# Expert retrieval: the mask products of a chunk issued in two halves, one group of expert rows behind each half

## The chip, the cores and the metric

The kernel runs on one core of one Trainium2 chip. The metric is the device time of one execution in microseconds (us), lower is better. Three runs of the kernel before took 1929.24 us in the median (1924.55 to 1931.2).

## The reference, cut to what matters

The whole program is four layers on x of shape 2 x 1024 x 256 (2048 tokens, 256 features); each layer adds `ffn(cond(x))` to x. The change touches only the feed-forward part of layer 0, a retrieval from 4096 experts by product keys:

```
q = (rmsnorm(x) @ w_q.T)                        # 8 heads, two halves of 128
s1, i1 = top_k(sim with keys half 0, 8)         # per token and head
s2, i2 = top_k(sim with keys half 1, 8)
fs, pk = top_k(s1[:, None] + s2[None, :], 8)    # 8 of 64 sums
fi = i1 * 64 + i2 at pk                         # 64 experts per token in all
hidden = gelu(xn . expert_down[fi]) * relu(fs)
out = sum over the 64 of hidden * expert_up[fi]
```

Nothing is gathered in this kernel. For each block of tokens all 4096 products with `expert_down` are taken, passed through gelu, and multiplied by a matrix of weights that is zero but for the 64 chosen experts of a token; a dense product with `expert_up` follows.

## The kernel before, in words

The program is a row of stages, each a block of code for every engine, one after the other. The stage of the change is `peer`. It walks over 8 blocks of 256 tokens (NPB = 8, PB = 256). Of a block there are:

- *Expert rows* (`act_rows`, L430 to L438, TensorE): the 4096 products per token, 32 slices j of 128 experts. Two slices are a *group* (16 groups, NGRP). The group is 4 matmuls in the source and 8 pairs of weight load and matmul in the trace, since each fp32 matmul is two. They use the whole array, 128x128, with 256 columns. ScalarE takes gelu of a group from one of two PSUM buffers into `hg` (L508).
- *Mask products* (`weigh`, L440 to L453, TensorE): the matrix of weights. A *chunk* is 16 token pairs (PAIRS), 8 chunks a block (CHUNKS), so 2 groups to a chunk (GPC). For each pair, the one-hot masks `am` and `bm` are contracted over the 64 slots of a token on quarters of the array, 64x64 with 32 columns: 64 matmuls in the source, 128 pairs of load and matmul in the trace. The result lies in `ps_w`, which has a single buffer.
- *Masks*: VectorE builds `bm` and `am` by comparison (`build`, L650 and L652) three chunks ahead in a ring of four; GpSimd multiplies `bm` by the slot's weight (L563).
- *The multiplication by the weights*: VectorE multiplies 1024 elements of `hg` per partition by the whole of `ps_w` once a chunk (L682) and signals `p_done`.
- *Up product* (L474, TensorE): 64 matmuls in the source, 128 pairs in the trace, 128x128 with 256 columns, then the sum with x on VectorE (L658).
- *Routing* of a later block: `scores` (L416, TensorE), `pick` (L584 to L639, VectorE), `turn` (two transposes, L426 and L427) and `keep` (ScalarE, L514 to L516), after which `build` may read the slots.

The order on each engine is written out by hand; semaphores tie them. TensorE in `work(i)` goes through the chunks of block i: before a chunk's mask products it waits for `a_done`, `b_done` (the masks) and `p_done` (L444: the multiplication of the chunk before has read `ps_w`), adds to a semaphore that marks the start (L445), issues the mask products, signals `w_ready`, and then issues two groups of the expert rows of block i + 1. After chunk 7 it issues the scores of block i + 2 (where there is one), waits for the last `p_done` and issues the up product. VectorE, per chunk: build the masks of three chunks later, then wait for `w_ready` and multiply. In block 0 it also does two parts of `pick` of block 1 in each chunk, and TensorE has the scores of block 1 behind chunks 0 and 4. In blocks 1 to 5 `pick` runs during the up product. Block 6 has no routing left, and block 7 no expert rows: there only mask products stand between the waits. Blocks 1 to 4 are two turns of a hardware loop; the others are written out.

Of the kernel before, what the change touches and what calls it, by code (L numbers as in the profile page):

```python
# [66 lines left out]
class Stage:  # L67
# [18 lines left out]
    def sem(self, name):  # L86
        return self.ctx.enter_context(self.nc.semaphore(f"{self.name}_{name}"))
# [253 lines left out]
PAIRS = 16  # L341
# [3 lines left out]
CPT = CHUNKS // PT  # L345
RING = 4
NGRP = NJ // 2
GPC = NGRP // CHUNKS


def peer(nc, a, g):
# [7 lines left out]
    with Stage(nc, "peer") as st:  # L359
# [31 lines left out]
        a_done, beq_done, b_done = sem("a_done"), sem("beq_done"), sem("b_done")  # L391
        w_begun, w_ready, p_done, o_ready, x_done = sem("w_begun"), sem("w_ready"), sem("p_done"), sem("o_ready"), sem("x_done")
# [3 lines left out]
        @block.sync  # L396
        def _(sp):
            def load_x(i):
                sp.dma_start(xin[:], a["x"][:, :, bass.ds(i * PB, PB)]).then_inc(xload, 16)

            load_x(0)
            with sp.Fori(1, NPB) as r:
                sp.wait_ge(x_done, r)
                load_x(r)

        @block.tensor
        def _(pe):
            def scores(i, t):

                n = i * PT + t  # L410
                if t == 0:
                    pe.wait_ge(xt_done, i + 1)
                pe.wait_ge(sim_read, n)
                for h in range(2):
                    for c in range(C):
                        mm = pe.matmul(ps_s[:, h, :], xt[:, c, t * P:(t + 1) * P],  # L416
                                       g.key_map[:, c, h * BLK:(h + 1) * BLK], start=(c == 0), stop=(c == C - 1))
                mm.then_inc(sim_ready, 1)

            def turn(i, t):  # L420

                n = i * PT + t
                pe.wait_ge(codes_done, n + 1)
                pe.wait_ge(kept, n * 6)
                flat = codes[:].rearrange("p a k -> p (a k)")
                pe.transpose(ps_t[:, 0:P], flat[:, 0:P], g.ident[:])  # L426
                pe.transpose(ps_t[0:SLOTS, P:2 * P], flat[:, P:P + SLOTS], g.ident[:]).then_inc(turned, 1)  # L427

            def act_rows(i, group):

                n = i * NGRP + group
                pe.wait_ge(gelu_done, n)
                for r in range(2):
                    j = 2 * group + r
                    for c in range(C):
                        mm = pe.matmul(ps_h[group % 2][:, r, :], down[:, c, j * P:(j + 1) * P],  # L436
                                       g.x[:, c, bass.ds(i * PB, PB)], start=(c == 0), stop=(c == C - 1))
                mm.then_inc(h_ready, 1)  # L438

            def weigh(i, c):  # L440
                n = i * CHUNKS + c
                pe.wait_ge(a_done, n + 1)
                pe.wait_ge(b_done, n + 1)
                pe.wait_ge(p_done, n + 1)  # L444
                pe.sem_inc(w_begun, 1)  # L445
                for m in range(PAIRS):
                    for k in range(P // WC):
                        of = slice(WC * k, WC * k + WC)
                        for z in range(2):
                            token = slice(64 * z, 64 * z + 64)  # L450
                            mm = pe.matmul(ps_w[of, z, m, :], am[c % RING][token, m, of], bm[c % RING][token, m, :],  # L451
                                           start=True, stop=True)
                mm.then_inc(w_ready, 1)  # L453

            def work(i, half, first=False, more=True, route=True):

                for c in range(CHUNKS):
                    weigh(i, c)
                    if more:
                        if first and c % CPT == 0:  # L460
                            scores(i + 1, c // CPT)
                        for group in range(c * GPC, (c + 1) * GPC):
                            act_rows(i + 1, group)
                            if first and group == NGRP // 2 + 1:
                                turn(i + 1, 0)
                            if not first and group == 2:
                                turn(i + 1, 1)
                if route:
                    scores(i + 2, 0)
                pe.wait_ge(p_done, i * CHUNKS + CHUNKS + 1)  # L470
                pe.wait_ge(x_done, i)
                for c in range(C):
                    for j in range(NJ):
                        mm = pe.matmul(ps_o[:, c, :], up[:, j, c * P:(c + 1) * P], hg[half][:, j, :],  # L474
                                       start=(j == 0), stop=(j == NJ - 1))
                        if c == 0 and j == NJ // 2 and first:
                            turn(i + 1, 1)
                        if c == 0 and j == NJ // 2 and route:
                            scores(i + 2, 1)
                        if c == 1 and j == 2 and route:  # L480
                            turn(i + 2, 0)
                mm.then_inc(o_ready, 1)

            scores(0, 0)
            for group in range(NGRP):
                act_rows(0, group)
                if group == 3:
                    scores(0, 1)
                if group == 5:
                    turn(0, 0)  # L490
            turn(0, 1)
            work(0, 0, first=True)
            with pe.Fori(0, NPB // 2 - 2) as r:
                work(r * 2 + 1, 1)
                work(r * 2 + 2, 0)
            work(NPB - 3, 1)
            work(NPB - 2, 0, route=False)
            work(NPB - 1, 1, more=False, route=False)
# [1617 lines left out]
```

## Time and profile before

| what | us |
|---|---|
| median of three runs | 1929.24 |
| the profiled execution's own time | 1929.26 |
| its span | 1927.6 |
| TensorE busy | 1757.1 (91%) |
| TensorE weight loads busy | 1097.1 (57%) |
| VectorE busy | 943.0 (49%) |
| ScalarE busy | 374.6 (19%) |
| GpSimd busy | 305.4 (16%) |
| stretch of the stage, first mask product to the end of the last sum | 194.7 to 853 |

The table says how busy each engine is over the whole span, which is a mean over stages with different limits. What counts here is the stretch from 194.7 to about 853 us, and in it the stretches in which the mask products and the expert rows alternate. Loads and matmuls of TensorE are two rows of the trace (PEld and PE) that overlap, and matmul ends are modelled; starts are better to reckon with than busy times. A row's first number is its start from the begin of the span, the second how long the merged instructions last from the first start to the last end.

### The profile page before, as it was taken

What the parts mean: (1) busy time and instruction counts of PE and PEld (TensorE: products, weight loads), DVE (VectorE), ACT (ScalarE), POOL (GpSimd) and SP (SyncE); (2) the same over time, 40 slices, a digit from 0 to 9 for tenths busy, and PEclk for the clock granted to TensorE, in tenths of its full rate; (3) what the DMA queues carried; (4) which work ended last, traced back from release to release, by engine and by line L of the source; (5) the groups of instructions that cost most, each with busy time, mean ns of one, the idle gap of its engine ahead of it and who ended that gap; (6) DMA issues with size and microseconds to landing.
All of it is one profiled execution on the core that took longest, in us unless ns stands there. A gap on an engine that the chain in (4) does not pass through costs nothing. (4 is left out here: it accounts for less than half of the span.)

```text
span 1927.6 us, 32039 instructions
## 1 busy us (share of the span) xinstructions
PE 1757.1 (91%) x13350; PEld 1097.1 (57%) x13350; DVE 943.0 (49%) x2520; ACT 374.6 (19%) x635; POOL 305.4 (16%) x150
## 2 busy tenths in 40 slices
PE   5879789999999999778799998999999976998998
PEld 2347678887888888764344443444444455447443
DVE  1326888768687785407311111111114497236676
ACT  2222111120111201001011111111113639133200
POOL 0000413151331514200394000000000000004000
PEclk9988899999999999789899999999999988999999
DMA  7000000000000000025310001200001044000000
GB/s 305 33 0 6 2 2 8 2 9 8 2 8 2 9 7 3 8 79 232 150 47 1 0 0 73 123 0 0 0 0 55 0 155 139 6 0 1 6 17 22
DMA packets 20043, 73.33 MB, mean 38 GB/s; under 512 B 3530, under 2 KB 8130, under 8 KB 17090
## 3 DMA queue, kind: packets, MB, share of 16 engines
q1 hardware_dynamic: 19906, 71.37, 9.9%
q8 instruction: 102, 1.67, 0.4%
q14 instruction: 35, 0.29, 0.0%
HBM read 69.26 MB, written 2.10 MB: 37 GB/s over the span
## 5 line engine op out<-in xcount | busy, mean ns | idle before, releaser
L563 POOL TENSOR_TENSOR peer_bm<-peer_bm,peer_slots 128x512 f32<-128x512 f32 x64 | 193.9, 3029 | 609.1 <-DVE peer_bm L650 609.1
L436 PE MATMUL peer_ps_h<-all_x,layer_down 128*128 128x256 f32 (+1 forms) x1024 | 241.3, 390 | 0.4 <-issue 0.4
L474 PE MATMUL peer_ps_o<-peer_hg,layer_up 128*128 128x256 f32 x1024 | 226.6, 382 | 1.5 <-DVE peer_hg L682 1.5
L474 PEld LDWEIGHTS peer_ps_o<-peer_hg,layer_up 128*128 128x128 f32 x1024 | 195.9, 192 | 33.3 <-issue 5.2
L436 PEld LDWEIGHTS peer_ps_h<-all_x,layer_down 128*128 128x128 f32 x1024 | 192.9, 193 | 28.4 <-issue 2.5
L1129 DVE SCALAR_TENSOR_TENSOR skills_hid<-skills_ps_u,all_pair_w,skills_act_g 128x512 f32<-128x512 f32 x64 | 48.0, 751 | 294.7 <-PE skills_ps_u L1091 294.7
L451 PE MATMUL peer_ps_w<-peer_bm,peer_am 64*64 64x32 f32 x8192 | 144.5, 227 | 31.9 <-DVE peer_hg L682 25.1
L451 PEld LDWEIGHTS peer_ps_w<-peer_bm,peer_am 64*64 64x64 f32 x8192 | 137.1, 144 | 52.1 <-issue 52.1
L508 ACT ACTIVATE peer_hg<-peer_ps_h 128x512 f32<-128x512 f32 x128 | 76.4, 597 | 371.7 <-PE peer_ps_h L436 371.7
L652 DVE TENSOR_TENSOR peer_am<-all_iota_a,peer_slots 128x2048 f32<-128x2048 f32 x64 | 146.2, 2285 | 0.0
L1108 ACT ACTIVATE skills_act_g<-skills_ps_g 128x512 f32<-128x512 f32 x96 | 57.3, 597 | 438.0 <-PE skills_ps_g L1091 438.0
L1091 PE MATMUL skills_ps_u<-all_x,skills_w 128*128 x256 | 120.3, 593 | 0.0
L1091 PE MATMUL skills_ps_g<-all_x,skills_w 128*128 x256 | 120.3, 593 | 0.0
L1078 PE MATMUL skills_acc<-skills_hid,skills_w 128*128 128x512 f32 x256 | 120.0, 593 | 0.0
L682 DVE TENSOR_TENSOR peer_hg<-peer_ps_w,peer_hg 128x1024 f32<-128x1024 f32 x64 | 78.2, 1222 | 77.6 <-PE peer_ps_w L451 77.5
L1310 POOL PARTITION_ALL_REDUCE quant_alltop<-quant_top x5 | 2.1, 424 | 588.9 <-DVE quant_top L1214 588.9
L1129 DVE SCALAR_TENSOR_TENSOR skills_hid<-skills_ps_u,skills_act_g 128x512 f32<-128x512 f32 x32 | 22.1, 692 | 142.5 <-PE skills_ps_u L1091 142.5
L1091 PEld LDWEIGHTS skills_ps_g<-all_x,skills_w 128*128 128x128 f32 x256 | 48.8, 191 | 61.1 <-issue 61.1
L1078 PEld LDWEIGHTS skills_acc<-skills_hid,skills_w 128*128 128x128 f32 x256 | 48.8, 191 | 61.1 <-issue 61.1
L1091 PEld LDWEIGHTS skills_ps_u<-all_x,skills_w 128*128 128x128 f32 x256 | 48.8, 191 | 61.1 <-issue 61.1
L1326 PE MATMUL quant_ps_m<-layers_y,layer_qw 128*128 128x512 f32 x192 | 82.8, 593 | 0.7 <-ACT layer_qw L1369 0.7
L1091 PE MATMUL skills_ps_g<-all_x,four_skill 128*128 x128 | 63.7, 622 | 17.2 <-DMA four_skill<-in_skills 10.7
(288 smaller groups left out, 2228.0 us busy)
## 6 DMA issues: line engine op xcount, KB each, us to landing
quant_w<-in_l_w SPq DMA_DIRECT2D x64, 256.0 KB, 4.3
lora_w<-in_l_w SPq DMA_DIRECT2D x8, 1024.0 KB, 8.7
four_skill<-in_skills SPq DMA_DIRECT2D x2, 3072.0 KB, 12.9
skills_w<-in_skills SPq DMA_DIRECT2D x2, 3072.0 KB, 15.1
skills_w<-in_skill_shared SPq DMA_DIRECT2D x2, 3072.0 KB, 22.0
layer_down<-in_down SPq DMA_DIRECT2D x1, 4096.0 KB, 24.3
layer_up<-in_up SPq DMA_DIRECT2D x1, 4096.0 KB, 33.5
swiglu_w<-in_cond SPq DMA_DIRECT2D x2, 1541.0 KB, 8.2
```

Source lines behind the costliest of these rows:

```text
L436: mm = pe.matmul(ps_h[group % 2][:, r, :], down[:, c, j * P:(j + 1) * P], g.x[:, c, bass.ds(i * PB, PB)], start=(c == 0), stop=(c == C - 1))
L451: mm = pe.matmul(ps_w[of, z, m, :], am[c % RING][token, m, of], bm[c % RING][token, m, :], start=True, stop=True)
L474: mm = pe.matmul(ps_o[:, c, :], up[:, j, c * P:(c + 1) * P], hg[half][:, j, :], start=(j == 0), stop=(j == NJ - 1))
L508: act.activation(hg[half][:, 2 * group:2 * group + 2, :], ps_h[group % 2][:], ACT.Gelu).then_inc(gelu_done, 1)
L563: pool.tensor_tensor(bm[c % RING][:], bm[c % RING][:], slots[half][:, 2, c * PAIRS:(c + 1) * PAIRS].unsqueeze(2).to_broadcast([P, PAIRS, WJ]),
L652: dve.tensor_tensor(am[c % RING][:], g.iota_a[:].unsqueeze(1).to_broadcast([P, PAIRS, P]), slots[half][:, 0, col].unsqueeze(2).to_broadcas ...
L682: dve.tensor_tensor(acts, ps_w[:].rearrange("p z m j -> p z j m"), acts, ALU.mult).then_inc(p_done, 1)
L1078: mm = pe.matmul(acc[k][c][:], w_down[s][:, m, c * P:(c + 1) * P], hid[j % 4][:], start=(s == 0 and m == 0), stop=(s == 2 and m == M2 - 1))
L1091: mm = pe.matmul(bank[:], weight[:, c, m * P:(m + 1) * P], g.x[:, c, bass.ds((b * BPB + k) * BLK, BLK)], start=(c == 0), stop=(c == C - 1))
L1108: act.activation(act_g[j % 2][:], ps_g[j % 2][:], ACT.Gelu_apprx_tanh).then_inc(gelu_done, 1)
L1129: dve.scalar_tensor_tensor(out=hid[j % 4][:], in0=ps_u[j % 2][:], scalar=scale, in1=act_g[j % 2][:], op0=ALU.mult, op1=ALU.mult).then_inc( ...
L1326: mm = pe.matmul(ps_m[n % n_ring][:], wt[z][:, c, m * P:(m + 1) * P], g.y[:, c, q * BLK:(q + 1) * BLK], start=(c == 0), stop=(c == C - 1))
```

## The change

`weigh` takes a `part`, 0 or 1. Part 0 has the waits, the mark of the start and the mask products of pairs 0 to 7; part 1 has the products of pairs 8 to 15 and the signal `w_ready`. In `work`, part 0, one group, part 1, one group take the place of all products and two groups. The scores in block 0 move from behind the whole of a chunk's products to behind part 0. The number of instructions that TensorE computes with is as before, and so is all code of the other engines.

```diff
-            def weigh(i, c):
+            def weigh(i, c, part):
                 n = i * CHUNKS + c
-                pe.wait_ge(a_done, n + 1)
-                pe.wait_ge(b_done, n + 1)
-                pe.wait_ge(p_done, n + 1)
-                pe.sem_inc(w_begun, 1)
-                for m in range(PAIRS):
+                if part == 0:
+                    pe.wait_ge(a_done, n + 1)
+                    pe.wait_ge(b_done, n + 1)
+                    pe.wait_ge(p_done, n + 1)
+                    pe.sem_inc(w_begun, 1)
+                for m in range(part * PAIRS // GPC, (part + 1) * PAIRS // GPC):
...
-                mm.then_inc(w_ready, 1)
+                if part == GPC - 1:
+                    mm.then_inc(w_ready, 1)
...
                 for c in range(CHUNKS):
-                    weigh(i, c)
-                    if more:
-                        if first and c % CPT == 0:
-                            scores(i + 1, c // CPT)
-                        for group in range(c * GPC, (c + 1) * GPC):
+                    for part in range(GPC):
+                        group = c * GPC + part
+                        weigh(i, c, part)
+                        if more:
+                            if first and c % CPT == 0 and part == 0:
+                                scores(i + 1, c // CPT)
                             act_rows(i + 1, group)
                             if first and group == NGRP // 2 + 1:
                                 turn(i + 1, 0)
                             if not first and group == 2:
                                 turn(i + 1, 1)
```

## Rows read from the trace of the kernel before

**Rows 1.** The page's 40 slices: TensorE's busy tenths and granted clock.
```profile
PE   5879789999999999778799998999999976998998
PEclk9988899999999999789899999999999988999999
```

**Rows 2.** Busy time by stretch: chunks of block 0, of block 2, of block 7.
```profile
core 0: us, PE busy (x) PEld busy (x) DVE busy (x) ACT busy (x) POOL busy (x), PEclk, DMA share, GB/s
194.70:273.40 78.70, 64.31 (x1179) 50.80 (x1179) 69.60 (x209) 11.89 (x24) 30.30 (x10) 0.89 0.01 2
385.40:430.53 45.13, 45.13 (x1155) 39.57 (x1155) 33.14 (x28) 10.66 (x22) 24.23 (x8) 1.00 0.03 9
786.22:822.25 36.03, 23.20 (x1025) 22.39 (x1024) 21.44 (x17) 0.00 (x0) 12.12 (x4) 0.68 0.04 11
```

**Rows 3.** Waits of TensorE's matmuls, blocks 1 to 6: total, times, longest.
```profile
PE peer_ps_w L451 <- issue: 4.0, 4, 1.8
PE peer_ps_w L451 <- DVE peer_hg L682: 0.9, 1, 0.9
```

**Rows 4.** Timeline of one chunk, block 2: start, length, engine, line, idle before.
```profile
402.57 1.97 PEld L451 LDWEIGHTS peer_ps_w<-peer_bm,peer_am 64*64 64x64 f32 x128 [0.33 <-issue]
404.58 3.32 PEld L436 LDWEIGHTS peer_ps_h<-all_x,layer_down 128*128 128x128 f32 x16
404.71 1.23 DVE L682 TENSOR_TENSOR peer_hg<-peer_ps_w,peer_hg 128x1024 f32<-128x1024 f32 x1 [1.62 <-PE peer_ps_w L451]
405.85 0.68 DVE L650 TENSOR_TENSOR peer_bm<-all_iota_a,peer_slots 128x512 f32<-128x512 f32 x1
406.45 2.29 DVE L652 TENSOR_TENSOR peer_am<-all_iota_a,peer_slots 128x2048 f32<-128x2048 f32 x1
408.23 1.96 PEld L451 LDWEIGHTS peer_ps_w<-peer_bm,peer_am 64*64 64x64 f32 x128 [0.33 <-issue]
...
425.18 1.96 PEld L451 LDWEIGHTS peer_ps_w<-peer_bm,peer_am 64*64 64x64 f32 x128 [0.33 <-issue]
```

**Rows 5.** The sequencer's wait and mark of that chunk, 403 to 408.2 us.
```profile
L444 PEldq EVENT_SEMAPHORE  x1: 51/51/51, 406.0 to 406.0; - x1
...
L445 PEldq EVENT_SEMAPHORE  x1: 51/51/51, 406.1 to 406.1; - x1
```

**Rows 6.** Timeline, up product of block 6 and first chunks of block 7.
```profile
758.29 27.60 PEld L474 LDWEIGHTS peer_ps_o<-peer_hg,layer_up 128*128 128x128 f32 x128
786.22 1.96 PEld L451 LDWEIGHTS peer_ps_w<-peer_bm,peer_am 64*64 64x64 f32 x128 [0.33 <-issue]
788.43 1.23 DVE L682 TENSOR_TENSOR peer_hg<-peer_ps_w,peer_hg 128x1024 f32<-128x1024 f32 x1 [1.34 <-PE peer_ps_w L451]
789.94 1.99 PEld L451 LDWEIGHTS peer_ps_w<-peer_bm,peer_am 64*64 64x64 f32 x128 [1.76 <-issue]
```

**Rows 7.** Timeline, a chunk of block 7 at the lower clock.
```profile
801.70 3.54 PEld L451 LDWEIGHTS peer_ps_w<-peer_bm,peer_am 64*64 64x64 f32 x128 [1.64 <-issue]
```

**Rows 8.** Timeline of block 0, chunks 1, 4 and 5.
```profile
208.15 2.85 PEld L451 LDWEIGHTS peer_ps_w<-peer_bm,peer_am 64*64 64x64 f32 x118 [4.67 <-issue]
212.18 5.00 PEld L436 LDWEIGHTS peer_ps_h<-all_x,layer_down 128*128 128x128 f32 x16
214.43 1.21 DVE L682 TENSOR_TENSOR peer_hg<-peer_ps_w,peer_hg 128x1024 f32<-128x1024 f32 x1
...
242.27 1.15 DVE L584 MAX8 peer_s<-peer_ps_s 128x8 f32<-128x64 f32 x8 [5.92 <-PE peer_ps_s L416]
...
245.41 0.27 PE L426 MATMUL peer_ps_t<-all_ident,peer_codes 128*128 128x128 f32 x1
...
247.62 0.69 DVE L650 TENSOR_TENSOR peer_bm<-all_iota_a,peer_slots 128x512 f32<-128x512 f32 x1 [2.03 <-ACT peer_slots L516]
```

**Rows 9.** Timeline, first chunk of the hardware loop's second turn.
```profile
469.15 0.66 PEld L451 LDWEIGHTS peer_ps_w<-peer_bm,peer_am 64*64 64x64 f32 x34 [1.89 <-issue]
```

**Rows 10.** Timeline, last sum of the stage and first load of the next.
```profile
852.39 0.69 DVE L658 TENSOR_TENSOR all_x<-peer_ps_o,peer_xin 128x512 f32<-128x512 f32 x1 [30.19 <-PE peer_ps_o L474]
853.56 0.34 SPq L768 DMA_DIRECT2D lora_a_rows<-in_l_a  x1
```

## The prediction

> **What bounds the kernel now.** I read the page's slices first. TensorE's digits are 9 over most of the retrieval stage, from the sixth slice to the sixteenth, with a granted clock of 9 tenths or more [rows 1]. The busy time by stretch then tells which part of the stage has slack. In the chunks of block 2 TensorE's matmul row is busy for 45.13 of 45.13 us at clock 1.00, VectorE for 33.14. In block 0 VectorE is busy 69.60 of 78.70 us and TensorE 64.31, at clock 0.89. In block 7, without expert rows, neither is full [rows 2]. The waits say the same: over blocks 1 to 6 TensorE's mask products wait 4.0 us for issue and 0.9 us for VectorE, in 480 us [rows 3]. So in blocks 1 to 6 whatever lengthens TensorE's stream lengthens the kernel, and a wait that is taken away would give nothing, since there is none. Nor does a later stage take it up: the next stage's first load is issued at 853.56 us, after the stage's last sum at 852.39 [rows 10].
>
> Last, the timeline of one chunk [rows 4]. A chunk begins with its first mask load at 402.57 us; the next begins at 408.23 and the fourth after it at 425.18: (425.18 - 402.57) / 4 = 5.652 us a chunk. How much of that is the products themselves?
> - Mask products: 128 loads in 1.96 us, the last of which lasts about 0.135, so one starts every (1.96 - 0.13) / 127 = 0.0144 us, and 128 take 1.84 us.
> - Expert rows: the up product has the same shape, and its 128 loads take 27.60 us [rows 6], so (27.60 - 0.19) / 127 = 0.2158 us each, and 16 take 3.45 us.
> - Together 5.30 us. The remaining 0.36 us (5.652 - 1.843 - 3.453 = 0.356) is what it costs to go from expert rows to mask products and back, once a chunk. On the way in the loads stand still for 0.33 us; on the way out the first expert load comes at 404.58, about 0.17 after the last mask load, and the second one a little early, which gives some back.
>
> **The change part by part.**
>
> *The added pair of edges, blocks 1 to 6.* The chunk was products, two groups; it becomes half, group, half, group. Each chunk with expert rows gets one more edge of each kind. That is 6 blocks x 8 chunks = 48 pairs in the part where TensorE sets the time. What does an added pair cost? The trace has no edge without the waits ahead of it, so I bound it. Lower end: nothing, and even 0.1 us of gain if only the early second load remained. Upper end for the edge: the 0.36 us of today. I take 0.356. The reason: the sequencer passes the wait for `p_done` at 406.0 us and the mark at 406.1 [rows 5], while the mask loads that follow start at 408.23. It is 2.1 us ahead, so neither wait nor mark holds up the loads; the 0.33 us is the array's own, between 128x128 work and 64x64 work. The same 0.33 us stands ahead of block 7's first mask products, behind the up product [rows 6]. 48 x 0.356 = 17.1 us.
>
> The Trainium skill, page "TensorEngine Tiling (Array Packing)", section "Key Properties", has a rule that speaks against this change: changing the tiling mode, not just the tile, drains the TensorE. By it the added edges cost as much as the present ones, since no wait is part of their price; the trace's equal gaps agree. If instead the gap were the waits', the added edges would be nearly free, and that is a rival below.
>
> *The wait for `p_done` gets closer.* Now two groups lie between the end of the products and the next ones; afterwards one. Queued behind the wait are the mask products, and behind them everything of TensorE. The multiplication starts 0.13 us after the first expert load (404.71 against 404.58) and takes 1.23; where TensorE waits for it, in block 7, the mask loads start 789.94 - (788.43 + 1.23) = 0.28 us after its end [rows 4, 6]. So with one group the loads can start at the earliest 0.13 + 1.23 + 0.28 = 1.64 us after the group's first load. The group itself and the edge take 1.73 + 0.2 = 1.92. The wait is hidden with 0.28 us to spare. The mask loads lose the sequencer's lead of 2.1 us; if the lead were needed whole, a chunk would be 3.65 - 1.92 = 1.73 us longer, 83 us in all. But in block 7 they start with no lead and take 1.99 against 1.96 [rows 6]: 0.03 us. 48 x 0.03 = 1.4 at most; I take 0.5. Behind chunk 7 of block 6 there are no scores to cover the wait before the up product: 1.64 against 1.62, nothing.
>
> VectorE can be in time: its cycle is 1.23 + 0.68 + 2.29 = about 4.1 us, and it idles 1.62 us before each multiplication [rows 4], which now comes in a cycle of 6.0.
>
> *Block 0.* VectorE's chain sets the time, and its cycle of about 7.7 us or more covers the added edges where TensorE runs at the upper clock (half 0.9, group 1.7, half 0.9, edges 0.7: 4.3 us from `p_done` to `w_ready`, against 6.3 us until VectorE wants it). At the lower one (1.2 GHz) it doesn't. 128 mask loads take 3.54 us there [rows 7], and 8 expert rows 2 x 1.73 = 3.5. In chunk 1 the products start at 208.15 us, with a stall inside; now they end at about 212, afterwards at 208.15 + 3.5 + 3.5 + about 0.6 of edges = 215.8, and the multiplication, at 214.43 today, comes at about 216 [rows 8]. +1.5 us. In chunk 4 the path runs through TensorE to the transposes at 245.41 and by ScalarE to the build at 247.62, which VectorE waits for 2.03 us: both halves, both groups and the scores all lie before them, so the added pair counts: +0.4. The scores come half a chunk's products earlier and shorten the 5.92 us wait, but the build behind them waits for the transposes anyway: 0. I take +2 for the block, bounds 0 (lower clock in other places) and +5 (three chunks like chunk 1).
>
> *Loop edge.* At the loop's second turn the mask products stall 1.89 us for issue after 94 loads [rows 9]. A group behind half of them gives the instructions more time to arrive. Four such stalls cost 4.0 us [rows 3]; bounds 0 to -4, and I take -1.
>
> *Block 7 and the up products*: same instructions in the same order, 0.
>
> **Sum**: 17.1 + 0.5 + 2 - 1 = 18.6 us, on 1929.26 of the profiled execution, which is the median of the runs (1929.24) to 0.02: 1947.9, say 1948 us, 1.0% slower. Likeliest case's own range: 1943 (block 0 at 0, stalls at -3.5) to 1953 (block 0 at +5, lead at 1.4).
>
> **The rivals.**
> - *Half a price.* Only one direction of the edge repeats: the way out (about 0.16 us of the 0.36) is plain, the way in is tied to the start of a chunk. 48 x 0.18 = 8.6, plus 1: 1939 us. For it: no edge without a wait is in the trace. Against it: the sequencer is long past the start of the chunk when the loads stand still [rows 5]. 8%.
> - *The wait takes over.* If `p_done` to mask loads took 0.6 us rather than 0.28 when the sequencer has been held, the slack of 0.28 would be gone and 0.3 us a chunk added: 48 x 0.3 = 14 more, 1962 us. It decides from 0.56 us up. Against: block 7's row, the very case. 5%.
> - *The gap is the waits' after all*, and added edges cost nothing: 1929 us, with block 0 and the stalls cancelling. 4%.
> - *Faster, by shorter bursts.* Mask products issue an instruction every 7 ns, and a burst of half the length gives issue time to catch up: the stalls (4.0 us) go [rows 3], and in chunk 4 of block 0 VectorE's wait of 5.92 us shortens by half of 3.54 us, 1.8. 1929.3 - 5.8 = 1923.5. It wins only if an added pair costs under 5.8 / 48 = 0.12 us. For it: the rows of stalls. Against: 0.36 stands in each chunk at full rate, with no stall. 3%.
> - The forecast: 80%.
>
> **How the numbers follow.** Range 1938 to 1954: it takes in the forecast with its bounds and the half price, and leaves out 1962, 1929 and 1923.5, 12%, and some of the tails. A measurement of this kernel can't tell less than about 0.3% (5.8 us) from no change. Slower by more than that: 80 + 8 + 5 = 93%; within it: 4%; faster: 3%.
>
> **What would show it.** Right: in the timeline of blocks 1 to 6 the mask loads come in runs of 64, an idle of 0.33 us ahead of both runs, an expert group of 8 loads between them, and the next chunk 6.01 us after; TensorE's wait for L682 stays near nothing there; blocks 1 to 6 are 17 us longer. Wrong: an idle of 0.1 or less ahead of the second run (half price or none); a wait for L682 in each chunk (the wait took over); chunk period at 5.65. Block 0 wrong if its chunks 0 to 7 take less than 78.7 us or over 84.

## The result and the profile after

The changed kernel takes 1945.01 us in the median of five runs (1942.3 to 1949.53), the kernel before 1929.24 (also five). The ratio, over all runs, is 1.009 with a 95% interval of 1.0069 to 1.0111: slower by 13 to 21 us. The forecast was 1948 us, range 1938 to 1954. The profiled execution is the median one, 1945.01 us with a span of 1943.3.

The page's slices, as in [rows 1]; the sixth to sixteenth lie in the stage:

```profile
PE   5878799999999999879799998999999977998998
PEclk9988899999999999888899999999999988998899
```

The eye finds nothing there. TensorE was at 9 before and is at 9 now; that is what a stream made longer by small gaps looks like in busy tenths, since matmul ends are modelled and cover the gaps. The stretches answer to [rows 2]: the chunks of block 0, of block 2, of block 7.

```profile
194.97:274.12 79.15, 64.83 (x1179) 48.50 (x1179) 69.73 (x210) 11.89 (x24) 30.30 (x10) 0.91 0.01 2
388.57:439.53 50.96, 50.96 (x1162) 41.16 (x1162) 33.32 (x28) 11.27 (x23) 24.23 (x8) 1.00 0.03 9
798.24:835.71 37.47, 25.22 (x1025) 24.36 (x1025) 21.69 (x17) 0.00 (x0) 12.12 (x4) 0.61 0.04 10
```

Block 2's row is from its first mask load to its first up product; in the kernel before that stretch is 385.40 to 433.75, 48.35 us (it holds also the 3.2 us of scores that [rows 2] leave out). So +2.6 us in 8 chunks, with clock and matmul count the same. Block 0 has +0.5 us, block 7 +1.4 at a clock of 0.61 against 0.68. Block 7's chunks took 36.03 and 34.87 us in two traces of the kernel before, and 37.25 in experiment 4, where their order is unchanged too, so its 1.4 us can't be put down to the change.

The timeline of one chunk (start, length, engine, line), to be laid beside [rows 4]:

```profile
403.74 1.02 PEld L452 LDWEIGHTS peer_ps_w<-peer_bm,peer_am 64*64 64x64 f32 x64 [0.33 <-issue]
404.80 1.59 PEld L436 LDWEIGHTS peer_ps_h<-all_x,layer_down 128*128 128x128 f32 x8
404.94 1.22 DVE L685 TENSOR_TENSOR peer_hg<-peer_ps_w,peer_hg 128x1024 f32<-128x1024 f32 x1 [1.95 <-PE peer_ps_w L452]
...
406.73 1.02 PEld L452 LDWEIGHTS peer_ps_w<-peer_bm,peer_am 64*64 64x64 f32 x64 [0.33 <-issue]
407.79 1.59 PEld L436 LDWEIGHTS peer_ps_h<-all_x,layer_down 128*128 128x128 f32 x8
409.72 1.02 PEld L452 LDWEIGHTS peer_ps_w<-peer_bm,peer_am 64*64 64x64 f32 x64 [0.33 <-issue]
```

The load at 403.74 is part 1 of a chunk, the one at 406.73 part 0 of the next, the one at 409.72 that chunk's part 1. Both stand behind an idle of 0.33 us, though part 1 has no wait ahead of it. A chunk takes 2 x (406.73 - 403.74) = 5.98 us against 5.65. The multiplication ends at 404.94 + 1.22 = 406.16 and part 0 could load from 406.44 on (+0.28, [rows 6]); it does at 406.73. The wait for `p_done` is hidden with 0.29 us left. In the later chunks of block 7 the loads follow the multiplication's end by 0.22 and 0.23 us, which would leave 0.35. The sequencer shows the lead that is gone: it passes the last wait at 406.2 and the mark at 406.3 (in [rows 5] it was 2.1 us ahead, now 0.4).

```profile
L445 PEldq EVENT_SEMAPHORE  x1: 51/51/51, 406.2 to 406.2; - x1
...
L446 PEldq EVENT_SEMAPHORE  x1: 51/51/51, 406.3 to 406.3; - x1
```

**Where the time went.** The chunks of blocks 1 to 6, first mask load to first up product, add up to 305.3 us after and 294.0 before: only 11.3 us. Block 5 of the first trace explains why that isn't 15.7, the 48 added pairs of edges at 0.328 us each (experiment 2). Its row, and the same block in a second trace of the unchanged kernel (see the last experiments):

```profile
629.02:681.38 52.36, 50.30 (x1163) 42.43 (x1163) 33.25 (x29) 11.26 (x23) 24.23 (x8) 0.97 0.03 8
```
```profile
630.80:679.31 48.51, 48.39 (x1162) 41.04 (x1162) 33.14 (x29) 11.27 (x23) 24.24 (x8) 1.00 0.03 9
```

The 3.9 us of a stall and the lower clock behind it do not belong to the order of instructions, since they aren't there again. Against the second trace the six blocks have 305.3 - 290.1 = 15.2 us more. Block 0 gives 0.3 to 0.5. Block 7 and all behind it move by some 1 to 3 us either way from trace to trace, of one kernel too.

### The profile page after: what moved, and what is told of

It reads as the page before. It is cut to its first block and busy times, and to the rows that moved or that the text cites. A ratio compares the mean times of both kernels' runs of the same rounds, so it can differ in the third digit from the quotient of the medians.

```text
span 1943.3 us, 32039 instructions
## 1 busy us (share of the span) xinstructions
PE 1781.0 (92%) x13350; PEld 1098.5 (57%) x13350; DVE 943.9 (49%) x2520; ACT 374.7 (19%) x635; POOL 305.6 (16%) x150
## 5 line engine op out<-in xcount | busy, mean ns | idle before, releaser
L436 PE MATMUL peer_ps_h<-all_x,layer_down 128*128 128x256 f32 (+1 forms) x1024 | 253.9, 393 | 0.0
L436 PEld LDWEIGHTS peer_ps_h<-all_x,layer_down 128*128 128x128 f32 x1024 | 187.3, 191 | 27.7 <-issue 1.9
L452 PE MATMUL peer_ps_w<-peer_bm,peer_am 64*64 64x32 f32 x8192 | 153.8, 227 | 29.2 <-DVE peer_hg L685 27.2
L1094 PE MATMUL skills_ps_g<-all_x,four_skill 128*128 x128 | 63.9, 624 | 17.1 <-DMA four_skill<-in_skills 10.6
```

The costliest lines, as they stand in the source:

```text
L1094: mm = pe.matmul(bank[:], weight[:, c, m * P:(m + 1) * P], g.x[:, c, bass.ds((b * BPB + k) * BLK, BLK)], start=(c == 0), stop=(c == C - 1))
```

## The experiments

**1. The waits without the edge.** In the kernel before, the waits and the mark a second time, in the middle of the products:

```diff
                 for m in range(PAIRS):
+                    if m == PAIRS // 2:
+                        pe.wait_ge(a_done, n + 1)
+                        pe.wait_ge(b_done, n + 1)
+                        pe.wait_ge(p_done, n + 1)
+                        pe.sem_inc(w_begun, 1)
```

> The kernel before, with a second set of the three waits and the mark in the middle of each chunk's mask products, and no expert rows there: TensorE's waits without a change of the array's mode. Theory (the gap of 0.33 us is the array's switch between 128x128 and 64x64 work): the 128 mask loads still come in one run of 1.96 us, a chunk stays at 5.65 us, 1929 us in all. Rival (the gap belongs to the waits and the mark ahead of the products): an idle of about 0.3 us in the middle of each run, 64 x 0.3 = 19 us in all, of which the 48 chunks of blocks 1 to 6 count in full: 1944 us or more.

Measured: 1934.22 us against 1928.51, ratio 1.0027 (1.0008 to 1.0046). The timeline, block 2:

```profile
400.16 1.83 PEld L456 LDWEIGHTS peer_ps_w<-peer_bm,peer_am 64*64 64x64 f32 x117 [0.33 <-issue]
402.25 0.31 PEld L456 LDWEIGHTS peer_ps_w<-peer_bm,peer_am 64*64 64x64 f32 x11 [0.26 <-issue]
402.60 3.32 PEld L436 LDWEIGHTS peer_ps_h<-all_x,layer_down 128*128 128x128 f32 x16
406.25 1.96 PEld L456 LDWEIGHTS peer_ps_w<-peer_bm,peer_am 64*64 64x64 f32 x128 [0.33 <-issue]
```

The run of 128 loads is unbroken at its middle, as at 406.25, and the edge ahead of it is what it was. The next chunk's first load comes at 411.90, 5.65 us after 406.25. The waits alone don't make the gap: the rival is out. They aren't quite free, though. The program is slower by 1.5 to 9 us, and single bursts lose a little elsewhere, as the 0.26 us behind load 117. Of the 5.7 us between the medians, block 0 has 1.7 in the trace (80.50 against 78.80 in the second trace of the kernel before) and blocks 1 to 6 have 2.0 (292.1 against 290.1). That the extra sequencer instructions do it by the supply of instructions is a guess.

**2. Twice the added edges.** The products in parts of 6, 5 and 5 pairs. `GAPS` names, behind each part, the group of the chunk and its slices:

```diff
+CUTS = (0, 6, 11, 16)
+GAPS = (((0, (0,)),), ((0, (1,)),), ((1, (0, 1)),))
...
-                for m in range(part * PAIRS // GPC, (part + 1) * PAIRS // GPC):
+                for m in range(CUTS[part], CUTS[part + 1]):
```

> The mask products of a chunk in three parts (6, 5 and 5 pairs), half a group of expert rows behind the first and the second, one whole group behind the third. Two added pairs of edges a chunk instead of one, and the same distance to the wait for p_done as in the changed kernel. Theory (each pair of edges costs 0.33 us whatever stands between): chunks of 5.65 + 2 x 0.33 = 6.30 us, 48 x 0.65 = 31 us, and 1 to 2 us in block 0: 1961 us. Rival (the cost is that of splitting at all, or of the waits, and not of each edge): 1945 us, as the changed kernel. Rival (cost by the length of what stands between, as if an interrupted stream had to refill): less than 0.33 for the short gaps, 1950 to 1955 us.

Measured: 1960.11 us against 1928.51, ratio 1.0148 (1.0116 to 1.0181). Block 2:

```profile
394.69:448.28 53.59, 53.59 (x1162) 41.22 (x1162) 33.32 (x28) 11.27 (x23) 24.22 (x8) 1.00 0.03 8
```
```profile
407.52 0.79 PEld L456 LDWEIGHTS peer_ps_w<-peer_bm,peer_am 64*64 64x64 f32 x48 [0.33 <-issue]
408.36 0.73 PEld L439 LDWEIGHTS peer_ps_h<-all_x,layer_down 128*128 128x128 f32 x4
409.42 0.67 PEld L456 LDWEIGHTS peer_ps_w<-peer_bm,peer_am 64*64 64x64 f32 x40 [0.33 <-issue]
```

48.34, 50.96, 53.59 us for none, one and two added pairs a chunk: steps of 2.62 and 2.63, that is 0.328 us a pair, behind 4 expert loads as behind 8 or 16. The cost is by the edge, and not by how many expert loads lie between. Block 0 took 81.63 us, 2.9 more than in the kernel before, where 1 to 2 were expected: with two added pairs VectorE's chain no longer covers them.

What stands directly ahead of the edge does matter. Behind the two transposes, which have 128 columns where the expert rows have 256, the idle is 0.20 us:

```profile
404.58 0.11 PEld L429 LDWEIGHTS peer_ps_t<-all_ident,peer_codes 128*64 128x64 f32 x1
404.88 0.67 PEld L456 LDWEIGHTS peer_ps_w<-peer_bm,peer_am 64*64 64x64 f32 x40 [0.20 <-issue]
```

And where the work changes but the 128x128 shape stays, there is no gap. In the kernel before, the last expert loads of block 6 end at 754.94 + 3.32 = 758.26 us and the up product loads from 758.29 [rows 6]:

```profile
754.94 3.32 PEld L436 LDWEIGHTS peer_ps_h<-all_x,layer_down 128*128 128x128 f32 x16
```

So the gap goes with the change from 128x128 to 64x64. Whether it is a price of the change itself, or the rest of the last wide product that the next load can't overlap, no run separates.

**3. The same edges, the wait brought too close.** The whole group first, half a group behind the last part. The edit against experiment 2:

```diff
-GAPS = (((0, (0,)),), ((0, (1,)),), ((1, (0, 1)),))
+GAPS = (((0, (0, 1)),), ((1, (0,)),), ((1, (1,)),))
```

> The same parts and the same number of edges as the thirds with the long gap last, but the whole group behind the first part and half a group behind the second and the third, so that only half a group stands between the last product and the wait for p_done. Theory: the mask loads can start at the earliest 1.64 us after the half group's first load (0.13 until the multiplication, 1.23 for it, 0.28 until the loads), and the half group takes 0.54 + 0.52 = 1.06: TensorE waits 0.58 us for L685's like in 7 of 8 chunks, 42 x 0.58 = 24 us more than the other thirds, 1985 us. Rival (the sequencer's lead matters beyond the wait itself, so that mask loads run slower when it is gone): more than 24 us, and loads further apart than 14 ns in a part. Rival (the wait has more slack than I reckon): no wait, 1961 us.

Measured: 1990.93 us, ratio 1.0306 (1.0268 to 1.0345), 31 us more than experiment 2. The waits of TensorE over blocks 1 to 6 (total, times, longest), and one wait:

```profile
PE peer_ps_w L456 <- DVE peer_hg L690: 22.6, 42, 2.5
```
```profile
416.85 0.73 PEld L439 LDWEIGHTS peer_ps_h<-all_x,layer_down 128*128 128x128 f32 x4
416.99 1.22 DVE L690 TENSOR_TENSOR peer_hg<-peer_ps_w,peer_hg 128x1024 f32<-128x1024 f32 x1 [2.84 <-PE peer_ps_w L456]
...
418.43 0.82 PEld L456 LDWEIGHTS peer_ps_w<-peer_bm,peer_am 64*64 64x64 f32 x48 [0.85 <-issue]
```

42 waits, as counted. The loads start 418.43 - 416.85 = 1.58 us after the half group's first (1.64 was reckoned; the loads follow the multiplication's end by 0.22 and not 0.28), and 48 loads take 0.82 against 0.79: 0.03 for the lost lead. Six blocks x (57.47 - 53.59) is 23.3 us, near the 24 expected. Between the two profiled executions lie 28.8 us: blocks 1 to 6 have 25.0 of them (347.5 against 322.5 us), block 7 has 2.1 and block 0 0.6. So the arithmetic of the slack holds, and in a steady chunk with a whole group behind the products there is none to pay.

**4. Block 0 alone.** In the changed kernel, the blocks behind block 0 take all 16 pairs at once:

```diff
-                        weigh(i, c, part)
+                        if first:
+                            weigh(i, c, part)
+                        elif part == 0:
+                            weigh(i, c, 0, 1)
```

> The changed order in block 0 alone; blocks 1 to 6 as before. Theory (VectorE's chain covers the added edges in block 0, the trace of the changed kernel has 0.5 us more there): block 0's first mask products to first up product in 78.7 to 79.5 us, 1929 to 1930 us in all. Rival (block 0 is a cost of its own, as I forecast it at 2 us with the lower clock in chunk 1): 80 us or more for that stretch.

Measured in a single run: 1926.08 us beside a median of 1928.51. Block 0:

```profile
194.79:273.93 79.14, 64.74 (x1179) 48.41 (x1179) 69.72 (x210) 11.90 (x25) 30.28 (x10) 0.91 0.01 2
```

79.14 us, against 78.68 and 78.80 in the two traces of the kernel before: VectorE's chain covers most of the edges there.

**5 and 6. Fewer edges, and a second buffer.** The products of odd chunks go to the scores' PSUM buffer in blocks 1 to 7, which lets them run ahead of the multiplication. Experiment 6 is that alone; experiment 5 issues two chunks' products back to back besides, from block 1 on. Since the scores share the buffer, TensorE also waits for the multiplication ahead of them. The edit of experiment 5; in experiment 6 both branches of `groups` are as the first:

```diff
+        ps_w2 = ps_s[:].rearrange("p z (m j) -> p z m j", j=WJ)
...
+                odd = c % 2 == 1 and not first
...
-                pe.wait_ge(p_done, n + 1)
+                pe.wait_ge(p_done, n if odd or (c > 0 and not first) else n + 1)
+                if c == 1 and not first:
+                    pe.wait_ge(sim_read, NPB * PT if type(i) is int and i == NPB - 1 else i * PT + 2 * PT)
...
-                        for group in range(c * GPC, (c + 1) * GPC):
+                        if first:
+                            groups = range(c * GPC, (c + 1) * GPC)
+                        else:
+                            groups = range((c - 1) * GPC, (c + 1) * GPC) if c % 2 else ()
+                        for group in groups:
...
+                    if not first:
+                        pe.wait_ge(p_done, i * CHUNKS + CHUNKS + 1)
                     scores(i + 2, 0)
```

> Fewer edges instead of more. In blocks 1 to 7 the products of odd chunks go to the PSUM buffer of the scores, which is free while the chunks run, so that the wait for p_done is for the chunk before the last; in blocks 1 to 6 TensorE issues the products of two chunks back to back and then four groups. One pair of edges for two chunks instead of two. Theory (0.33 us a pair): two chunks in 11.30 - 0.33 = 10.97 us, 24 x 0.33 = 7.8 us less in blocks 1 to 6. In block 7, where each product waits for the multiplication before it, the two overlap: 5 chunks at VectorE's 4.1 us and three at 2 to 3.6 us instead of 36 us, some 7 us less. In all 1929 - 15 = 1914 us. Rival (edges don't count by number, only the splitting cost): blocks 1 to 6 as before, 1922 us.

> The second buffer alone, chunks and groups in the order of the kernel before. Theory: blocks 1 to 6 as before (the wait was hidden there anyway, 5.65 us a chunk), block 7 some 7 us shorter: 1922 us, so that the difference from the kernel with products back to back, 7.8 us, is that of 24 pairs of edges. Rival (the earlier p_done is worth something in blocks 1 to 6 too): less than 5.6 us a chunk.

Measured beside a median of 1930.65 us: experiment 6 takes 1919.84, ratio 0.9939 (0.9925 to 0.9952), faster than both kernels. Experiment 5 takes 1947.76, ratio 1.009 (1.0068 to 1.0111), where I expected 1914. First experiment 6, block 2 and block 7:

```profile
385.04:433.36 48.32, 48.32 (x1162) 41.01 (x1162) 33.13 (x28) 11.26 (x23) 24.23 (x8) 1.00 0.03 9
780.22:809.04 28.82, 17.38 (x1025) 16.47 (x1024) 21.33 (x17) 0.00 (x0) 12.12 (x4) 0.94 0.05 14
```

Block 2 is as before, since no wait was there to take away; blocks 1 to 6 together take 288.2 us against 290.1, and the 1.9 us come nearly all from block 3 (49.77 against 51.10, see the loop edge below). Block 7 falls from 36.03 us to 28.82, with VectorE's 21.33 us now closer to the stretch and the clock at 0.94 for 0.68.

Then experiment 5. TensorE's waits over blocks 1 to 6, and two bursts of block 2:

```profile
PE peer_ps_s L456 <- issue: 20.7, 19, 2.3
```
```profile
401.13 1.96 PEld L456 LDWEIGHTS peer_ps_w<-peer_bm,peer_am 64*64 64x64 f32 x128 [0.33 <-issue]
403.06 1.99 PEld L456 LDWEIGHTS peer_ps_s<-peer_bm,peer_am 64*64 64x64 f32 x128
405.08 0.94 PEld L437 LDWEIGHTS peer_ps_h<-all_x,layer_down 128*128 128x128 f32 x5
406.96 5.80 PEld L437 LDWEIGHTS peer_ps_h<-all_x,layer_down 128*128 128x128 f32 x27 [0.93 <-issue]
413.09 2.09 PEld L456 LDWEIGHTS peer_ps_w<-peer_bm,peer_am 64*64 64x64 f32 x127 [0.33 <-issue]
...
418.96 0.94 PEld L456 LDWEIGHTS peer_ps_s<-peer_bm,peer_am 64*64 64x64 f32 x32 [2.38 <-issue]
```

The edges did what the theory says: from 401.13 to 413.09 are 11.96 us, less the stall of 0.93 it is 11.03 for two chunks, against 2 x 5.65 = 11.30. But a burst of 256 pairs, 512 instructions, stalls for issue, up to 2.4 us and 19 times in 24 bursts. The stall at 418.96 lies within one chunk's products, 32 loads before their end, where no wait stands. The clock falls behind it (0.91 over block 2's chunks, 57.96 us). The chunks of blocks 1 to 6 take 321.8 us in all against 290.1 in the second trace of the kernel before: some 40 us lost to win 7.8.

**7. Both.** Halves in the kernel of experiment 6.

> The second buffer together with the change's order (half, group, half, group). Theory (the added pair of edges costs 0.33 us whatever the waits for p_done do): the kernel with the buffer alone, 1919.8 us, plus 48 x 0.33 = 15.7 and 0.5 in block 0: 1936 us; blocks 1 to 6 at 50.96 us of chunks as in the changed kernel. Rival (part of the change's cost is the closer wait for p_done or the sequencer's lost lead, which the second buffer gives back): under 50.5 us a block, 1930 us or less.

Measured: 1934.96 us, ratio 1.0025 (1.001 to 1.004) to 1929.24, and 15.1 us over experiment 6's median (16.5 when each is set against the unchanged kernel timed beside it; 16.2 by the sizes so far). Block 2:

```profile
387.68:438.64 50.96, 50.96 (x1163) 41.16 (x1162) 33.33 (x28) 11.27 (x23) 24.22 (x8) 1.00 0.03 9
```

50.96 to the hundredth, with the wait for `p_done` a chunk further off; block 3, the loop's second turn, takes 50.96 here too. So in the steady chunks of the changed kernel the closer wait and the lost lead cost nothing.

**8. Does a longer pause spare the stalls?** In experiment 5 each expert product is computed twice into the same place:

```diff
-                for r in range(2):
+                for r in (0, 1, 0, 1):
```

> The kernel with products back to back, in which each expert row product is computed twice into the same place (same output, 13.8 us instead of 6.9 between two bursts of mask products). It asks why the bursts of 256 pairs stall for issue, 24.7 us in blocks 1 to 6. Theory (instructions are brought in blocks of 16 KB, 256 of them, and a burst of 512 in 3.7 us outruns them because the time between bursts is too short to fill what can be held): with twice the time between, and twice the instructions for it, the average rate falls from 58 to 41 instructions a us and most stalls go, under 6 us left. Rival (what can be held is less than a burst, so each burst stalls however long the pause): 20 us or more of issue waits again. In all about 1948 + 128 x 1.73 = 2169 us, less the stalls that go.

Measured in a single run: 2142.34 us, 27 less than the 2169 expected. Of that, 22 us are block 0's: its chunks grew by 5.4 us over experiment 5 (84.19 against 78.77) and not by 16 x 1.73 = 27.7, since VectorE's chain sets the time there. The waits over blocks 1 to 6:

```profile
PE peer_ps_s L456 <- issue: 22.4, 19, 2.0
PE peer_ps_w L456 <- issue: 3.0, 2, 1.9
```

My theory falls, the rival holds: with twice the pause the bursts stall 19 times again. The mean rates expected were too high, since two chunks have 512 + 64 loads and matmuls in experiment 5 and 512 + 128 here: 52 a us falls to 36. That strengthens the result. The kernel before runs at 51 a us, (256 + 32) / 5.65, with 4.0 and 1.9 us of issue waits in two traces, so it isn't the mean rate but the length of the burst that stalls.

Where the stalls fall says more. In block 6 of experiment 5 they end at 740.11, 752.27, 764.04 and 778.32 us; the two last stretches between them, with the matmuls (PE) and loads (PEld) in brackets:

```profile
752.26:764.03 11.77, 10.73 (x254) 9.47 (x254) 7.27 (x6) 2.39 (x4) 5.86 (x2) 1.00 0.01 3
764.03:778.31 14.28, 12.65 (x382) 11.39 (x382) 9.94 (x8) 2.39 (x4) 7.56 (x3) 1.00 0.02 4
```

That is 508 and 764 instructions, a few waits and marks short of 2 x 256 = 512 and 3 x 256 = 768. Block 6 of experiment 8 has 508 and 764 too, between stalls at 938.77, 956.97 and at 918.61, 938.77 us. The stalls keep step with blocks of 256 instructions, whatever the pause.

**Both kernels once more.**

> The changed kernel again, timed beside the others, with a second trace. Its mean difference from the kernel before is 48 x 0.33 = 15.7 us by the edges and 0.5 us in block 0: 1945 us. Chunks of blocks 1 to 6 at 50.96 us a block, and the first block of the loop's second turn again 2.7 us above that.

Measured: 1945.3 us against 1930.65, ratio 1.008 (1.0065 to 1.0094); blocks at 50.96 again, block 3 at 53.87.

> The kernel before, unchanged, for a second trace. If the 4.0 us that block 5 had more than its neighbours in the first trace (52.36 against 48.34 us: a stall for issue and the lower clock after it) belong to the order of instructions, they are there again; if they are chance, block 5 takes 48.3 to 48.6 us.

Measured in a single run: 1929.41 us. Block 5 takes 48.51 us (row above): its stall isn't there again. Block 3, the loop's second turn, takes 51.10, as 51.34 in the first trace: that loss stays.

## Why the prediction was right, step by step

- *TensorE sets the time in blocks 1 to 6.* Shown: each gap put in appears in full, 2.62 us a block for 8 pairs, and nothing for the waits that the second buffer takes away in the steady chunks. The one exception is the first chunk of block 3, below.
- *An added pair costs 0.356 us.* Mechanism right, size 8% high: 0.328 measured, 15.7 us for 17.1. I divided by a mean of 0.0144 us a mask load, but a burst's loads are closer at its start: 64 take 1.02 us, (1.02 - 0.13) / 63 = 0.0141. Two short bursts win back some of it. By the Trainium skill's rule ("TensorEngine Tiling (Array Packing)", "Key Properties"), a change of mode drains the array; experiments 1 and 2 agree, with 0.33 us ahead of each burst that has no wait and none in the middle of a burst that has. The 0.20 us behind the transposes was not in the prediction.
- *The half price.* Out by experiment 2 and by the equal 0.33 us ahead of part 1. The gap as the waits' cost is out by experiment 1, but for the small cost it found.
- *The wait for `p_done` is hidden with 0.28 us to spare.* Shown: 0.29 in the timeline, experiment 7 with no change, experiment 3 with the wait where the reckoning puts it. So the rival of the wait taking over is out. The lost lead, 0.5 us in the sum, showed as 0 in the changed kernel: a burst of 64 takes 1.02 us behind the wait and without it.
- *Block 0, +2 us.* The term that was mis-sized: +0.3 to +0.5 (79.15, 79.17 and 79.14 us in three traces, against 78.68 and 78.80). I let the lower clock last through chunk 1 as it did before. It didn't:

```profile
209.75 2.98 PEld L436 LDWEIGHTS peer_ps_h<-all_x,layer_down 128*128 128x128 f32 x8
213.06 1.02 PEld L452 LDWEIGHTS peer_ps_w<-peer_bm,peer_am 64*64 64x64 f32 x64 [0.33 <-issue]
```

 The group runs at the lower clock (granted 0.52 from 209.75 to 212.7 us), the second half already at the upper one (1.00 from 213.06 to 214.1), while in [rows 8] 16 expert loads took 5.00 us. The multiplication came at 214.70, against 214.43, and the block's first load 0.27 later too: nothing was added. In chunk 4 the scores came earlier (VectorE's wait for them fell from 5.92 to 5.12 us) and the build waited for the transposes all the same, at 248.35 against 247.62, 0.46 more when the block's later start is taken off: the 0.4 of the forecast.
- *The loop edge, -1 us.* This step failed. TensorE's own stall did go, as forecast: its waits for issue over blocks 1 to 6 fell from 4.0 and 1.9 us in two traces to 0.2 and 0. But block 3 stands 2.7 and 2.9 us over its neighbours after, and 3.0 and 2.8 before (51.34 and 51.10 against 48.34), so nothing was won. The prediction had the wrong engine. At the same place VectorE idles, 3.2 to 3.5 us in all twelve traces, with nothing that it waits for in all but one of them. Before, and after:

```profile
469.54 0.69 DVE L650 TENSOR_TENSOR peer_bm<-all_iota_a,peer_slots 128x512 f32<-128x512 f32 x1 [3.26 <-issue]
```
```profile
475.37 0.69 DVE L653 TENSOR_TENSOR peer_bm<-all_iota_a,peer_slots 128x512 f32<-128x512 f32 x1 [3.30 <-issue]
...
478.79 1.21 DVE L685 TENSOR_TENSOR peer_hg<-peer_ps_w,peer_hg 128x1024 f32<-128x1024 f32 x1
...
480.22 1.05 PEld L452 LDWEIGHTS peer_ps_w<-peer_bm,peer_am 64*64 64x64 f32 x64 [3.00 <-issue]
```

 The late build makes the multiplication late; it ends at 478.79 + 1.21 = 480.00, and the products of chunk 1, which wait for it, start 0.22 us later. Before, the 1.89 us stall of TensorE lay beside VectorE's idle, and behind it TensorE still stood 1.22 us ahead of its load at 474.39, for the multiplication that ended at 474.16. So by these rows taking TensorE's stall away alone could win nothing. The second buffer, which puts the wait a chunk further off, shows the parts: with it and the halves block 3 has nothing left over (50.96), with it and whole bursts it keeps TensorE's own stall, 1.45 us (49.77 against 48.32).
- *Faster, by shorter bursts.* Half of this rival came true: shorter bursts did end TensorE's stalls. It gave no time, for the reason just given, and an added pair costs 0.328 us, far over the 0.12 below which it would win.

With the measured sizes the sum is 15.7 + 0 + 0.5 + 0 = 16.2 us. Measured by the medians are 15.8 and 14.7 us, each against the unchanged kernel timed beside it, with intervals of 13 to 21 and 12.5 to 18 us. The forecast of 18.6 was as near as it was partly by luck: the 1 us for the loop edge that didn't come took off some of what the other three terms had too much.

## What to carry to other kernels

Count the changes between full-array and quarter-array matmuls in TensorE's stream as instructions of their own: a round trip costs about a third of a us here, it hides in the busy share, and it is read off by setting a period against load count times spacing. Merge such runs, but only up to what the instruction supply bears. A second buffer pays where the trace shows the wait: here in block 7 and at the loop's second turn, and not in the steady chunks. When an engine stalls for issue, see whether its neighbour stalls at the same place before you count the stall as a gain. And look at a second trace before a few us of one block are given a cause.

## What the runs showed that I had not expected

Instructions are a resource. The mask products use an instruction every 7 ns. Bursts of 256 instructions mostly pass, bursts of 512 stall up to 2.4 us, with a pause of 6.9 us between them or of 13.8. The queue of instructions shows how they come, over blocks 1 to 7 of experiment 5 (packets, MB):

```profile
q8 instruction: 71, 1.16, 0.9%
```

1.16 MB / 71 is 16 KB a packet. The Trainium skill ("Runtime: NRT & Kernel Launch", "Instruction fetch mechanics") says that each engine's instruction memory is refilled in 16 KiB blocks of 256 instructions; the packets agree, and so do the 508 and 764 instructions between stalls. It also calls the crossing of a block mostly hidden, which this stream of short matmuls contradicts with 20.7 us of stalls; the measurement decides. Its warning that a taken branch whose target isn't at hand costs a fetch fits VectorE's idle of 3.2 to 3.5 us at the hardware loop's second turn, in all twelve traces; no run takes the branch away, so this stays a reading. That the supply of instructions is what runs out in the long bursts is supported by experiments 5 and 8 and by the spacing of their stalls, but no run isolates it from the other things of the sequencer.
